# Two LSTMs on one core: PSUM divided again into ordered buffers, and GpSimd's products placed behind the compares

## The reference

```python
def step(carry, xt):
    h, c = carry
    g = xt @ Wx + h @ Wh + b
    i, f, gg, o = jnp.split(g, 4, axis=-1)
    c = sigmoid(f) * c + sigmoid(i) * tanh(gg)
    h = sigmoid(o) * tanh(c)
    return (h, c), None
...
m_from = lstm_last(base_emb[from_seq], seq_Wx, seq_Wh, seq_b)     # 64 steps, H = 64
m_to   = lstm_last(base_emb[to_seq],   seq_Wx, seq_Wh, seq_b)
x = concatenate([num_emb[nums], freq_emb[freqs]], axis=-1)        # 11 features, 32 steps, H = 8
feats = concatenate([goby, indel, matches, m_from, m_to, count_fwd, count_rev, nwf])
return relu(feats @ reduce_W + reduce_b)
```

## Time and profile before

| | |
|---|---|
| median of 3 runs | 2191.85 us (2182.32 to 2198.21) |
| the profiled execution | 2191.35 us, span 2189.6 us |
| PE busy | 1806.4 us (83%) |
| DVE busy | 1672.6 us (76%) |
| ACT busy | 1076.4 us (49%) |
| POOL busy | 1083.3 us (49%) |
| DMA | 593.97 MB, hardware queue 87.0% of 16 engines |

### The profile page before, as it was taken

How to read it: one execution, slowest core, us unless ns; L and a number is a source line. 1 busy time by engine, 2 the same in 40 slices (tenths; PEclk the granted TensorE clock), 3 DMA queues, 4 the chain that set the end, 5 groups by cost and what they waited for, 6 DMA issues and landing times. The chain is left out here.

```text
span 2189.6 us, 63997 instructions
## 1 busy us (share of the span) xinstructions
PE 1806.4 (83%) x27396; PEld 767.8 (35%) x27396; DVE 1672.6 (76%) x1284; ACT 1076.4 (49%) x1459; POOL 1083.3 (49%) x477
## 2 busy tenths in 40 slices
PE   2278788888888888888888888888888888888884
PEld 1123333333333333333333333333333333333333
DVE  7178878887878787877788778888788877888771
ACT  2235455555545555555555545555455554555541
POOL 7358754545444445444444544544454444454551
PEclk9589999999999999999999999999999999999996
DMA  6789899999989999999999898899989998999962
GB/s 171 178 244 273 272 283 282 290 302 286 284 284 284 289 282 291 282 287 285 277 287 288 280 281 285 292 283 288 272 286 303 284 285 274 298 287 288 296 217 52
DMA packets 248101, 593.97 MB, mean 271 GB/s; under 512 B 56036, under 2 KB 158220, under 8 KB 206860
## 3 DMA queue, kind: packets, MB, share of 16 engines
q1 hardware_dynamic: 245259, 589.73, 87.0%
q0 software_dynamic: 2560, 0.15, 0.8%
HBM read 536.95 MB, written 7.54 MB: 249 GB/s over the span
## 5 line engine op out<-in xcount | busy, mean ns | idle before, releaser
L612 ACT ACTIVATE gate<-g_ps 128x1024 f32<-128x1024 f32 (+1 forms) x768 | 710.9, 940 | 232.9 <-PE g_ps L565 229.5
L645 POOL TENSOR_TENSOR seq_h<-gate,tanh_c 128x1024 f32<-128x1024 f32 x128 | 382.6, 2989 | 713.3 <-ACT tanh_c L639 713.2
L503 PE MATMUL e_ps<-hot,tab 128*32 128x512 bf16 x8448 | 531.6, 387 | 221.6 <-DVE hot L493 216.7
L493 DVE TENSOR_SCALAR hot<-low,cst 128x4096 bf16<-128x4096 bf16 x352 | 559.1, 1588 | 0.1
L512 DVE SCALAR_TENSOR_TENSOR kept<-high,cst,e_ps 128x1024 f32<-128x1024 bf16 x352 | 447.9, 1273 | 120.3 <-issue 106.7
L565 PE MATMUL g_ps<-seq_h,seq_wh 64*64 64x512 f32 x4096 | 535.5, 596 | 0.0
L619 POOL TENSOR_TENSOR ig<-gate 128x1024 f32<-128x1024 f32 x192 | 445.5, 2320 | 74.3 <-ACT gate L612 74.3
L503 PEld LDWEIGHTS e_ps<-hot,tab 128*32 128x32 bf16 x8448 | 195.3, 97 | 639.2 <-DVE hot L493 452.5
L459 DVE TENSOR_SCALAR seq_hot<-tok,cst 128x2048 bf16<-128x2048 bf16 x128 | 249.5, 1950 | 167.2 <-DMA tok<-seq_tokens 167.1
L538 ACT COPY nwf_x<-x_ps 128x256 f32<-128x256 f32 (+1 forms) x192 | 68.0, 354 | 505.0 <-PE x_ps L529 505.0
L473 ACT CAST seq_x<-sx_ps 128x512 bf16<-128x512 f32 x256 | 150.6, 588 | 250.1 <-PE sx_ps L467 248.9
(11 more groups left out here) (68 smaller groups left out, 981.7 us busy)
## 6 DMA issues: line engine op xcount, KB each, us to landing
low<-low_digits SPq DMA_DIRECT2D x352, 1024.0 KB, 8.0
high<-high_digits SPq DMA_DIRECT2D x1408, 64.0 KB
tok<-seq_tokens SPq DMA_DIRECT2D x128, 512.0 KB, 5.5
seq_h<-seq_h SPq DMA_DIRECT2D x256, 128.0 KB, 2.9
nwf_h<-nwf_h SPq DMA_DIRECT2D x64, 128.0 KB, 2.6
nwf_h<-nwf_h SPq DMA_DIRECT2D x64, 48.0 KB, 4.8
nwf_in<-in_r_nwf_numbers SPq DMA_DIRECT2D x1, 2816.0 KB, 13.7
nwf_in<-in_r_nwf_freqs SPq DMA_DIRECT2D x1, 2816.0 KB, 20.9
```

What stands on the lines that cost most here:

```text
L493: nc.vector.tensor_scalar(hot[:, p % HOT_RING, :, :].rearrange("p u c -> p (u c)"), low[:, p % LOW_RING, :, :].rearrange("p u c -> p (u c) ...
L503: last = nc.tensor.matmul(e_ps[32 * g:32 * g + 32, i, :], tab[:, part, 2 * m + ty, :], hot[:, p % HOT_RING, i, g * CH:(g + 1) * CH], start ...
L612: nc.scalar.activation(gates[g][:, n % 2, 0:2 * w].rearrange("p (b c) -> p b c", b=2), g_ps[g % 2][:, :, 0:w], GATES[g][1]).then_inc(gate_ ...
L645: nc.gpsimd.tensor_tensor(h_blocks(n)[:, 0:2, :].rearrange("p b c -> p (b c)"), gates[3][:, n % 2, 0:w], tanh_c[:, n % 2, 0:w], ALU.mult). ...
```

## The change

PSUM has the same eight banks in both kernels. Before, `g_ps` has four, `e_ps` two, `x_ps` and `sx_ps` one each. Now four banks make two buffers `ab`, which the gates g, i, o, the feature sets and the text inputs use in turn, in one fixed order (`USES`); `f_ps` has the two others. ACT takes the sigmoid of f in place in `f_ps`, DVE multiplies by c there, and the sum of that and `ig` goes to c in SBUF. The gate f of cell n waits for `add_c` of cell n - 1.

The high digits of a pair lie together in DRAM and come in one DMA of 2 KB rows for all partitions. The rings are 3, 4, 2 and 4 (low, high, hot, kept); loads run three pairs ahead, tokens are loaded two text inputs ahead of their compare, and inputs are made two text cells ahead. SP takes the swap of cell n - 2 at the head of cell n. The two matmul groups of a set are one (`set_input`), and so are the two halves of a text input.

```diff
-LOW_RING, HIGH_RING, HOT_RING, KEPT_RING, X_RING = 3, 3, 2, 2, 6
-AHEAD = 4
+        SETS_AT[_first + _k + 1] += [(_r, m) for m in range(NSETS)
+                                     if _j - _n <= NPAIRS * _r + SET_LAST[m] < _j]
+AHEAD, X_RING = 2, 3
+LOW_RING, HIGH_RING, HOT_RING, KEPT_RING = 3, 4, 2, 4
...
+USES = [("sx", _s) for _s in range(AHEAD)]
+for _n in range(NCELLS):
+    USES += [("x", _r, _m) for _r, _m in SETS_AT[_n]]
+    USES += [("gate", _n, 0), ("gate", _n, 1), ("gate", _n, 3)]
+    if later_seq(_n) is not None:
+        USES.append(("sx", later_seq(_n)))
+    if _n == LAST_SEQ + 1:
+        USES.append(("small",))
+USE = {x: n for n, x in enumerate(USES)}
...
-        high_dram = nc.dram_tensor("high_digits", [NWF_T, 2 * FEATURES, 4, CH], BF16, kind="Internal").ap()
+        high_dram = nc.dram_tensor("high_digits", [NWF_T, FEATURES, 4, 2, CH], BF16, kind="Internal").ap()
...
-        g_ps = [work.enter_context(nc.psum_tensor(f"g_ps{n}", [P, 2, CH], F32)) for n in range(2)]
+        ab = [work.enter_context(nc.psum_tensor(f"ab{n}", [P, 2, CH], F32)) for n in range(2)]
+        f_ps = work.enter_context(nc.psum_tensor("f_ps", [P, 2, CH], F32))
         e_ps = work.enter_context(nc.psum_tensor("e_ps", [P, 2, CH], F32))
-        x_ps = work.enter_context(nc.psum_tensor("x_ps", [P, 256], F32))
-        sx_ps = work.enter_context(nc.psum_tensor("sx_ps", [P, CH], F32))
...
+        def begin_use(pe, what):
+            at_least(pe, ab_done, USE[what] - 1)
+            return ab[USE[what] % 2]
+        def ab_is_done(eng, what):
+            at_least(eng, ab_done, USE[what] + 1)
...
-            for g in range(4):
-                sp.dma_start(high[32 * g:32 * g + 32, p % HIGH_RING, :, :],
-                             high_dram[step:step + 1, both, g, :]
-                             .to_broadcast([32, 2, CH])).then_inc(high_here[p % HIGH_RING], 16)
+            sp.dma_start(high[:, p % HIGH_RING, :, :].rearrange("p u c -> p (u c)"),
+                         high_dram[step, k, :, None, :, :].rearrange("g o u c -> g o (u c)")
+                         .to_broadcast([4, 32, 2 * CH])).then_inc(high_here[p % HIGH_RING], 16)
...
+        def set_input(pe, r, m):
+            first, last_pair = SET_LAST[m] - (SETS[m][1] == 2), SET_LAST[m]
+            at_least(pe, kept_ready, NPAIRS * r + last_pair + 1)
+            to = begin_use(pe, ("x", r, m))
+            n = SETS[m][1] * LANES
+            units = [(ty, k, q, p, i) for p in range(first, last_pair + 1)
+                     for i, (ty, _, quads) in enumerate(PAIRS[p]) for k, q in enumerate(quads)]
+            for ty, k, q, p, i in units:
+                last = nc.tensor.matmul(to[32 * q:32 * q + 32, 0, 0:n], cst[:, C_RED + 32 * ty:C_RED + 32 * ty + 32],
+                                        kept[:, (NPAIRS * r + p) % KEPT_RING, i, k * n:(k + 1) * n],
+                                        start=(ty == 0), stop=(ty == 1))
+            last.then_inc(ab_ready, 1)
...
-            at_least(pe, gate_done, 4 * n + g - 1)
+            if g == FORGET:
+                at_least(pe, c_ready, n)
+                bank = f_ps
+            else:
+                bank = begin_use(pe, ("gate", n, g))
...
+        def activate_f(act, n):
+            w = width(n)
+            act.wait_ge(f_ready, n + 1)
+            nc.scalar.activation(f_ps[:, :, 0:w], f_ps[:, :, 0:w], GATES[FORGET][1]).then_inc(f_done, 1)
...
+            dve.wait_ge(f_done, n + 1)
+            nc.vector.tensor_tensor(f_ps[:, :, 0:w], by_blocks(c_of(n), n), f_ps[:, :, 0:w],
+                                    ALU.mult).then_inc(c_scaled, 1)
         def add_c(dve, n):
-            w = 2 * width(n)
-            at_least(dve, c_scaled, n + 1)
-            at_least(dve, ig_ready, n + 1)
-            nc.vector.tensor_tensor(c_of(n), c_of(n), ig[:, n % 2, 0:w], ALU.add).then_inc(c_ready, 1)
+            w = width(n)
+            dve.wait_ge(c_scaled, n + 1)
+            dve.wait_ge(ig_ready, n + 1)
+            nc.vector.tensor_tensor(by_blocks(c_of(n), n), by_blocks(ig[:, n % 2, 0:2 * w], n), f_ps[:, :, 0:w],
+                                    ALU.add).then_inc(c_ready, 1)
...
                     sp.dma_start(dst, src).then_inc(s_late, 16)
+                for s in range(2, 4):
+                    load_tokens(sp, s)
                 for n in range(NCELLS):
-                    if later_seq(n) is not None:
-                        load_tokens(sp, later_seq(n))
-                    for i, p in enumerate(PAIRS_AT[n]):
-                        if p + PREFETCH < ALL_PAIRS:
-                            load_pair(sp, p + PREFETCH)
-                        if i == 0 and n:
-                            swap_h(sp, n - 1)
-                    if not PAIRS_AT[n]:
-                        swap_h(sp, n - 1)
+                    if n >= 2:
+                        swap_h(sp, n - 2)
+                    for p in PAIRS_AT[n]:
+                        load_later(sp, p + LOW_RING)
+                    s = later_seq(n)
+                    if s is not None and s + 2 < 2 * SEQ_T:
+                        load_tokens(sp, s + 2)
+                swap_h(sp, LAST - 1)
                 swap_h(sp, LAST)
...
-                    for p in pairs[:1]:
-                        compare_pair(dve, p)
+                    for p in pairs[:-1]:
+                        keep_wanted(dve, p)
+                        compare_pair(dve, p + 1)
+                    if len(pairs) == 1:
+                        keep_wanted(dve, pairs[0])
+                    if pairs and pairs[-1] + 1 < ALL_PAIRS:
+                        compare_pair(dve, pairs[-1] + 1)
                     if later_seq(n) is not None:
                         seq_compare(dve, later_seq(n))
-                    for i, p in enumerate(pairs[1:]):
-                        keep_wanted(dve, pairs[i])
-                        compare_pair(dve, p)
+                    if len(pairs) > 1:
+                        keep_wanted(dve, pairs[-1])
                     scale_c(dve, n)
                     add_c(dve, n)
...
                 for n in range(NCELLS):
+                    if later_seq(n) is not None:
+                        pool.wait_ge(seq_hot_ready, later_seq(n) + 1)
+                    input_product(pool, n)
                     if n:
                         new_h(pool, n - 1)
-                    input_product(pool, n)
...
                 for n in range(NCELLS):
+                    for r, m in SETS_AT[n]:
+                        store_x(act, r, m)
+                    activate(act, n, 0)
                     if n:
                         tanh_of(act, n - 1)
-                    activate(act, n, 0)
                     activate(act, n, 1)
-                    if n and PAIRS_AT[n - 1] and pair_ends(PAIRS_AT[n - 1][-1]):
-                        store_x(act, *pair_ends(PAIRS_AT[n - 1][-1]))
-                    activate(act, n, 2)
+                    activate_f(act, n)
+                    activate(act, n, 3)
                     if later_seq(n) is not None:
-                        seq_store_x(act, later_seq(n), 0)
-                    activate(act, n, 3)
-                    for p in PAIRS_AT[n][:-1]:
-                        if pair_ends(p):
-                            store_x(act, *pair_ends(p))
-                    if later_seq(n) is not None:
-                        seq_store_x(act, later_seq(n), 1)
+                        seq_store_x(act, later_seq(n))
...
                     pairs = PAIRS_AT[n]
-                    gate(pe, n, 0)
-                    gate(pe, n, 1)
                     for p in pairs[:1]:
                         look_up(pe, p)
-                    gate(pe, n, 2)
-                    if n:
-                        for p in PAIRS_AT[n - 1][-1:]:
-                            bring(pe, p)
+                    for r, m in SETS_AT[n]:
+                        set_input(pe, r, m)
+                    gate(pe, n, 0)
+                    for p in pairs[1:-1]:
+                        look_up(pe, p)
+                    gate(pe, n, 1)
+                    gate(pe, n, FORGET)
+                    if len(pairs) > 1:
+                        look_up(pe, pairs[-1])
+                    gate(pe, n, 3)
                     if later_seq(n) is not None:
-                        seq_lookup(pe, later_seq(n), 0)
-                    gate(pe, n, 3)
-                    for i, p in enumerate(pairs[1:]):
-                        look_up(pe, p)
-                        bring(pe, pairs[i])
-                    if later_seq(n) is not None:
-                        seq_lookup(pe, later_seq(n), 1)
-                    if n == LAST_SEQ:
+                        seq_lookup(pe, later_seq(n))
```

More of the change, by code:

```diff
@@ L49 @@
 GATES = [(2, ACT.Tanh), (0, ACT.Sigmoid), (1, ACT.Sigmoid), (3, ACT.Sigmoid)]
+FORGET = 2
 PAIRS = []
@@ L194, in store_pass @@
             else:
-                dram = low_dram if kind == "low" else high_dram
                 for r in range(4):
```

(35 more changed lines are left out.)

133 lines of the change are left out of this document (59 added, 74 removed).

## The result

The changed kernel takes 2699.29 us (median of 4 runs, 2690.20 to 2706.35), the kernel before 2195.03 us beside it (4 runs, 2182.32 to 2204.92): a ratio of 1.2299, with a 95% interval from 1.2222 to 1.2376. The forecast was 1999 us (1940 to 2125), a gain of 9%; what came is a loss of 23%.

A forecast was written before the change was run, and what follows sets the result against it. The prediction took a closed 10.88 us loop through POOL as the bound; without it, PE at 55.0 and DMA at 56.6 us gave 57.0 a round, 5.9 less, 192 us off 2191.35: 1999 us, range 1940 to 2125.

The forecast's parts named there:

- The loop that bounds the kernel before: Text cell: new_h, ig, a lengthened DVE compare, scale_c and add_c, tanh and handovers form a closed loop of 10.88 us.
- The chain through POOL goes: GpSimd: ig now precedes the previous cell's new_h, so the chain from sum to sum is 6.8 us against 10.88.
- the waits inside the compares go: VectorE: most of the 8.0 us a round that compares wait while POOL multiplies should go.
- tokens no longer wait: Token loads, issued two text cells before use: the compares' 5.1 us a round of waiting for DMA is gone.
- the hold: GpSimd's ig waits for the token compare, so compares run free of POOL's products; part of 8.0 us a round saved.
- three DMAs with 16 end marks each are spared: High digits' DMA: fewer, longer packets at 31 ns each save 3.7 us a round (0 to 7.4), leaving 54.2 us.
- If the queue can be kept between today's 92% and full: DMA queue: with 54.2 us of engine time, a round takes 54.2 to 58.9 us, middle 56.6.
- if packets took longer as the rate rose: DMA queue: a sign named in advance that would show the forecast wrong; no size given.
- rival 3: DMA at today's price: longer packets save nothing, share at most 96%, 60.3 us a round, 2105 us; chance 0.15.
- Rival 2: SP's queue: low loads stand behind a swap awaiting new_h; slower if landing exceeds 13.3 us; 2304 us; chance 0.11.
- Rival 1: All the way to PE: DMA keeps up at 322 GB/s, a round is 55.6 us, total 1952 us; chance 0.20.
- Rival 4: The hold doesn't work as said; another unseen closed loop of the same length bounds the kernel: 2191 us; chance 0.04.

The follow-up runs named there:

- e7: The kernel before, with only the first half of each pair's low digits loaded from the fourth pair on (result incomplete): 2161.34 us, ratio 0.9816.
- e6: e1 with only the first half of each pair's low digits loaded from the fourth pair on (result incomplete): 1900.79 us, ratio 0.8641.
- e12: e6 without GpSimd's wait for the token compare, its new order kept: 1898.52 us, ratio 0.8638.
- e3: e1 without GpSimd's wait for the token compare, its new order kept: 2172.02 us, ratio 0.9895.
- e15: e3 run again, unchanged, beside a kernel with tokens on 96 partitions: 2162.85 us, ratio 0.9816.
- e1: The changed kernel with a pair's high digits in four DMAs again, one for each quarter of the partitions: 2183.46 us, ratio 0.9914.
- e8: e5 with only the first half of each pair's low digits loaded from the fourth pair on (result incomplete): 2022.31 us, ratio 0.9195.
- e10: The changed kernel with each high-digit row stored four times, so the single DMA reads 16 source rows for 8 partitions each: 2219.89 us, ratio 1.0121.
- e5: e1 with GpSimd's order of before (new_h, then ig) and no wait for the token compare: 2186.51 us, ratio 0.9911.
- e11: e10 without GpSimd's wait for the token compare: 2214.31 us, ratio 1.0040.
- e13: e1 with each low load in two DMAs of 128 partitions, one for each half of the pair's digits: 2228.94 us, ratio 1.0134.

## Why the prediction was wrong

*The loop that bounds the kernel before* (10.88 us a cell): borne out. e7 took away 31% of the bytes and 1.8% of the time, and the cell kept its 10.87 us.

*The chain through POOL goes; the waits inside the compares go; tokens no longer wait*: right in direction, and mostly in size. Token compares take 765 ns in the mean and wait 0.5 us in all for their DMA; multiply and sum take 1.22 us where 1.27 was taken; pair compares stay at 1363 ns where 1.28 us was taken. PE's share of the loop in e6 is 98% where 97% was said. But the hold, on which the prediction laid the free compares, is worth no time: in e12 the order alone keeps them free, and in e3 and e15, where leaving it out lets them grow to 1424 and 1476 ns in the mean, the time is no longer for it.

*DMA: "three DMAs with 16 end marks each are spared"*: this is the step that failed, and it turned the sign. It takes the single DMA to be spread over 16 engines as the four were. It runs on four; even the marks spared are 60 a pair, not 48. By e1 against the changed kernel, that costs 2699 - 2183 = 516 us (by the ratios, (1.2299 - 0.9914) x 2195 = 524). The prediction looked at the packets of the new DMA, their number and length, and not at the dimension by which they are dealt out. None of its four rivals holds this mechanism.

*"If the queue can be kept between today's 92% and full"*: failed too, for 2183 - 1999 = 184 us. It took the engine time of a round, 54.2 us, as fixed and let only the share rise. The share did rise, to 1.01, but the rate stayed at 286 GB/s, since the bytes cost more engine time: over the whole execution it rose from 1905 to 2058 us, where the 3.7 us a round for spared packets would have taken off 120. The price of 31 ns for a packet as such is thus shown by no run. The 92% of the earlier trace rows was a queue already giving about all that it gives in this mixture; the 413 GB/s of the earlier trace rows were one slice of 1.25 us. The text named this among its signs of being wrong ("if packets took longer as the rate rose"), and rival 3, 0.15 at 2105 us, comes nearest to it; that rival took engine time at the price of before, while in e1 the price rose. Why it rose is open.

*Rival 2*, the slower one, had the landing as its hinge: beyond 13.3 us it decides. The landing came to 16.5 us. But not by SP's queue: e1 keeps the order of that queue as changed, with three issues more a pair, and takes 2183 us; and by the rival's own sum a landing of 16.5 us gives 2402, not 2699. So the 0.11 for a slower kernel was right in sign by another cause, which is luck. Its loop may carry part of the wait, which no run shows. *Rival 1* needed 322 GB/s, which no kernel here reached; with the fewer bytes of e6 the time fell below its 1952 us, to 1901. *Rival 4*, another loop of the same length, fell with e8 and e6: there the step of a cell and the time both go down.

## What to carry to other kernels

Before merging DMAs, look at the slowest dimension of both sides: here a source of 4 rows went over 4 engines and one of 16 rows over 16. A DMA on few engines can delay all other transfers while the mean share falls, so a falling share is no proof that the queue is free; the packets of a DMA beyond its rows, 132 against 128 here, tell how many engines it had. A DMA share of 0.92 was not a reserve of 8%: read the GB/s beside it, and test how much the queue holds back, for instance in a kernel that leaves a third of the bytes out. Where a wait is added to protect an instruction, try the new order without it first.

## What the runs showed of the hardware

- One DMA a pair with 4 source rows, 92.3 of 590 MB: 227 GB/s at a share of 0.74 for the whole queue, landing of another tile from 8.0 to 16.5 us, 23% more time. With 16 source rows (e10) or as four DMAs (e1): 288 and 286 GB/s, share 1.00 and 1.01.
- The full queue gave 285 to 292 GB/s where the low digits and tokens came to all 128 partitions by one DMA each (e1, e3, e5, e10, e11, e15), 280 with two for the low digits (e13), 271 with one tile on 96 partitions, 232 with the largest tile in two halves of 64 partitions in a row, and 288 with the same halves interleaved.
- TensorE's granted clock was 0.99 in the loop of e6, 0.95 in e1 and 0.88 in the changed kernel, where the same matmuls took 106 us longer in all than in the kernel before. It does not go by the busy share alone: from 400 to 1700 us the kernel before and e1 are both 87% busy, at 0.99 and 0.95.
